# First half's residual through ScalarE and one accumulating DMA, VectorE's single steps in front of its up additions, scales in three tiles

## The chip, the cores and the metric

The kernel runs on one core of one Trainium2 chip. The metric is the device time of one execution in microseconds (us); the median of repeated runs is what counts. The core has TensorE (PE) for matmuls into the eight PSUM banks, VectorE (DVE), ScalarE (ACT) and GpSimd (POOL) for elementwise work, and 16 DMA engines. DMAs are issued by SyncE (SP) and, where they add to what is there, by POOL.

## The reference

```python
x = x + attention(conv(x, cond, fside))            # before the stage of this case
f = dynamic_mix(x, cond)                           # 1x1 convolution with mixed weights
dequantize = (int_w - zeros) * scales              # one scale per group of 128 input rows
gate = silu(f @ gate_proj)                         # 512 -> 1792
up   = f @ up_proj                                 # 512 -> 1792
x = x + (gate * up) @ down_proj                    # 1792 -> 512
```

x has 32 x 32 = 1024 tokens of 512 values, float32. The change lies in the last four lines. The weights are integers less their zero points, held exactly in float16; each group of 128 inputs has its own scales, so a product over 512 inputs is four products over 128, each scaled and added in float32.

## The kernel before

After attention comes the feed-forward stage, the last 180 us. It is cut into 28 tiles (`TILES`): the 1792 hidden values in 14 blocks of 128 (`IC`), first for tokens 0 to 511 (the first half, tiles 0 to 13), then for tokens 512 to 1023 (tiles 14 to 27). Everything is transposed: values on partitions, 512 tokens along the row. Inputs and hidden values are split in a high and a low float16 part, so every product is two matmuls of 128x128 by 128x512. A tile n has:

- `gate(n)` on PE, four products, into banks 0 to 3. ACT scales products 0 and 2 out of PSUM (`scaled`, L1369), DVE scales 1 and 3 and adds them (`scaled`, L1929), POOL adds the two sums (`add_part`, L2191), ACT takes silu (`gate`, L1382).
- `up(n)` on PE, four products, into banks 0 to 2 and 7. ACT scales the first (`up_first`, L1397), DVE adds the other three (`up_added`, L1936). The next tile's gate products use the same banks, so PE's third gate product of tile n+1 waits for DVE's second up addition of tile n (L994).
- POOL multiplies the two (`hidden`), ACT and POOL split the result in high and low (`hidden_high`, `hidden_low`), and two tiles later (`LAG`) PE makes four products with the down weights (`down`, L1020). DVE scales and adds blocks 0 and 2 in `acc` (`down_added_to`, L1954); ACT scales blocks 1 and 3 into `dprod`, which has two buffers (`down_scaled`, L1415), and POOL issues a DMA that adds them in `acc` (`move_down`, L2207, 512 KB). Its landing is waited for by the next `move_down` and by ACT two tiles on, before it writes that buffer again (L1421).

Each engine runs its own list, written out by hand; in the loop over n the order is, on PE: gate(n), down(n-2) blocks 0 and 1, up(n), down(n-2) blocks 2 and 3. On DVE (L2011 to L2040): gate additions, down addition 0, up additions 1 and 2, down addition 2, up addition 3. On ACT (L1456 to L1479): down copy 3 of n-3, the two gate copies, down copy 1, `up_first`, `hidden_high`, silu. On POOL (L2281 to L2290): hidden(n-1), move_down(n-3), add_part(n), hidden_low(n-1). Between these stand single steps for the second half and for the residual:

- `mix_power(1)`, `hidden_bound(1)`, `hidden_diagonal(1)`, `hidden_power(1)` on DVE derive powers of two by which the second half's values are scaled. They stand at the head of tiles 5, 6 and 9.
- `rows_high` (ACT) and `rows_low` (DVE) split the second half's inputs, held in `fnat`, behind tiles 5, 7, 9, 11; SP then issues 16 transposing DMAs (L628), which `gate(14)` waits for.
- `turn_x(half, c)` (PE, L1059) transposes x into the bank `side`. For the second half ACT copies it into `acc` before any down product is there (`turned_x`). For the first half it is turned in tiles 16 and 17 and DVE adds it to the finished sums (`result`, L1977), block by block, and each turn waits for the one before it to be read (L1064). SP stores each block as it is done (L631).
- `later_scales` (ACT, tile 13) makes the second half's three sets of scales.

Of the kernel before, what the change touches and what calls it, by code (L numbers as in the profile page):

```python
# [11 lines left out]
KC = DM // P  # L12
# [15 lines left out]
MOVED = 16 * G  # L28
FIRST = 2
LAG = 2  # L30
ROWS = (5, 7, 9, 11)
TURN_X = (9, 10, 11, 12)
UNITS = 2 * HKV
EPS = 1e-6
MASKED = -1e30
# [56 lines left out]
def build(nc, x_in, xt_in, mask_in, fs_in, cond_in, cw_in, conv_in, wq_in, wkv_in, wo_in, w0_in, w1_in, w2_in, b2_in, mix_in, vec_in,  # L92
          gu_w_in, gu_z_in, gu_s_in, dn_w_in, dn_z_in, dn_s_in, const_in, sel_in, out):
    ctx = ExitStack()
    with ctx:
# [317 lines left out]
        l_acc = sem("l_acc")  # L413
        t_xT = sem("t_xT")
        a_xT = sem("a_xT")
        d_res = sem("d_res")


        norms = nc.dram_tensor("norms", (BQ, S, G, HQ), F32, kind="Internal").ap()
# [101 lines left out]
        def _(sp):  # L521
# [107 lines left out]
                                 fpair[S * b:S * b + S, t, :, :, :].rearrange("p k c n -> p (k c) n"),  # L629
                                 transpose=True).then_inc(l_fT, 16)  # L630
            for c in range(KC):  # L631
                sp.wait_ge(d_res, c + 1)
                sp.dma_start(out[:, c, tokens(0)], acc[:, 0, place(c), :]).then_inc(l_out, 16)
            for c in (0, 2, 1, 3):
                if c == 1:
# [8 lines left out]
        def _(pe):  # L644
# [392 lines left out]
            def last_downs():  # L1037

                n = TILES - 2
                pe.wait_ge(p_hlo, n + 1)  # L1040
                pe.wait_ge(d_res, KC)
                down_block(n, 1)
                pe.wait_ge(d_g, 2 * TILES)
                down_block(n, 0)
                pe.wait_ge(d_us, 3 * TILES - 1)
                down_block(n, 2)
                pe.wait_ge(d_us, 3 * TILES)
                down_block(n, 3)
                n = TILES - 1
                pe.wait_ge(d_hlo, 1)  # L1050
                pe.wait_ge(a_u, TILES)
                down_block(n, 1)
                down_block(n, 0)
                pe.wait_ge(d_dn, down_added(n - 2, 2))
                down_block(n, 2)
                pe.wait_ge(d_dn, down_added(n - 2, 3))
                down_block(n, 3)

            def turn_x(half, c):  # L1059

                if half == 0:
                    pe.wait_ge(a_xT, KC)
                    if c:
                        pe.wait_ge(d_res, c)  # L1064
                elif c:
                    pe.wait_ge(a_xT, c)
                else:
                    pe.wait_ge(d_y, HQ * UNITS)
                    pe.wait_ge(a_hm, 2)
                for t in range(HQ):  # L1070
                    last = nc.tensor.transpose(side[:, P * t:P * t + P], x[:, HQ * half + t, P * c:P * c + P], ident)
                last.then_inc(t_xT, 1)
# [21 lines left out]
            for n in range(2, TILES):  # L1094
                gate(n)
                if n >= LAG:
                    down(n - LAG, (0, 1))
                if n in (2, 3):
                    mix(2 * n)
                elif n in TURN_X:  # L1100
                    turn_x(1, n - TURN_X[0])
                elif n in (IC + LAG, IC + LAG + 1):
                    turn_x(0, 2 * n - 2 * IC - 2 * LAG)
                up(n)
                if n >= LAG:
                    down(n - LAG, (2, 3))
                if n in (2, 3):
                    mix(2 * n + 1)
                elif n == 4:
                    bound(1)  # L1110
                elif n == 5:
                    hidden_rows(1)
                elif n == 6:
# [7 lines left out]
        def _(act):  # L1121
# [247 lines left out]
            def scaled(n, g):  # L1369
                half, i = divmod(n, IC)  # L1370
                act.wait_ge(t_g, KC * n + g + 1)
                if i == 0 and g == 0:
                    act.wait_ge(a_fscl if half else p_fscl, 3 if half else 1)
                if n >= 2:
                    if g:
                        act.wait_ge(p_whole, n - 1)
                    else:
                        act.wait_ge(p_hlo, n - 1)
                A(part[:, n % 2, :] if g else whole[:, n % 2, :], bank[g][:, :], ACT.Copy,
                  scale=gscl[:, half, i, g:g + 1]).then_inc(a_g, 1)  # L1380
# [2 lines left out]
                act.wait_ge(p_whole, n + 1)  # L1383
                A(whole[:, n % 2, :], whole[:, n % 2, :], ACT.Silu).then_inc(a_silu, 1)

            def later_scales():
                act.wait_ge(p_fdown, 2)
                act.wait_ge(l_gus, 16)
                A(uscl[:, 1, :, :], gus[:, 1, :, :], ACT.Copy, scale=fdown[:, 1:2]).then_inc(a_fscl, 1)
                A(gscl[:, 1, :, :], gus[:, 0, :, :], ACT.Copy, scale=finv[:, 1:2]).then_inc(a_fscl, 1)  # L1390
                A(dsc[:, 1, :, :], dscl[:, :, :], ACT.Copy, scale=hdown[:, 1:2]).then_inc(a_fscl, 1)

            def hidden_scale(half):
                act.wait_ge(t_hx, 2 * half + 2)
# [2 lines left out]
            def up_first(n):  # L1397
                half, i = divmod(n, IC)
                act.wait_ge(t_u, KC * n + 1)
                if n == 0:  # L1400
                    act.wait_ge(p_fscl, 2)
                if n >= 2:
                    act.wait_ge(p_h, n - 1)
                A(exact[:, n % 2, :], up_bank(n, 0)[:, :], ACT.Copy, scale=uscl[:, half, i, 0:1]).then_inc(a_u, 1)  # L1404
# [10 lines left out]
            def down_scaled(n, c):  # L1415
                half, i = divmod(n, IC)
                act.wait_ge(t_dn, down_done(n, c))
                if n == TILES - 1:
                    act.wait_ge(p_acc, 1)
                elif n >= 3 and c == 1:  # L1420
                    act.wait_ge(l_acc, down_moved(n - 2))  # L1421
                A(dprod[:, n % 2, c // 2, :] if n else acc[:, 0, place(c), :], down_bank(n, c)[:, :], ACT.Copy,
                  scale=dsc[:, half, i, c:c + 1]).then_inc(a_dn, 1)
# [32 lines left out]
            for n in range(2, TILES):  # L1456
                if LAG < n <= DIRECT + LAG:
                    down_scaled(n - LAG - 1, 3)
                scaled(n, 0)
                if n == 3:  # L1460
                    mix_out(5)
                elif n == 4:
                    mix_out(7)
                scaled(n, 2)
                if n >= LAG:
                    down_scaled(n - LAG, 1)
                up_first(n)
                hidden_high(n - 1)
                if n in (2, 3):
                    mix_out(2 * n)  # L1470
                elif n in ROWS:
                    rows_high(ROWS.index(n))
                if n == 7:
                    hidden_scale(1)
                elif n in TURN_X:
                    turned_x(n - TURN_X[0])
                elif n == IC - 1:
                    later_scales()
                gate(n)  # L1479
            down_scaled(TILES - 2, 1)  # L1480
            hidden_high(TILES - 1)
# [5 lines left out]
        def _(dve):  # L1487
# [489 lines left out]
            def result(c):  # L1977

                dve.wait_ge(t_xT, KC + c + 1)
                if c % 2:  # L1980
                    dve.wait_ge(l_acc, down_moved(IC - 1))
                else:
                    dve.wait_ge(d_dn, down_added(IC - 1, c))
                V.tensor_tensor(acc[:, 0, place(c), :], side[:, :], acc[:, 0, place(c), :], ALU.add).then_inc(d_res, 1)

            probs_sum(UNITS - 1)
            mix_max(1)
            mix_max(2)
# [20 lines left out]
            add_outputs(UNITS - 1, 1, 3)  # L2009
            dve.wait_ge(p_fscl, 3)  # L2010
            for n in range(2, TILES):  # L2011
                if n == 5:
                    mix_power(1)
                    hidden_bound(1)
                elif n == 6:
                    hidden_diagonal(1)
                elif n == 9:
                    hidden_power(1)
                scaled(n, 1)
                if n in (IC + LAG + 1, IC + LAG + 2):  # L2020
                    result(2 * n - 2 * IC - 2 * LAG - 1)
                scaled(n, 3)
                if n >= LAG:
                    down_added_to(n - LAG, 0)
                if n == 3:
                    mix_max(4)
                    mix_max(5)
                elif n == 4:
                    mix_max(6)
                    mix_max(7)  # L2030
                if n in (IC + LAG, IC + LAG + 1):
                    result(2 * n - 2 * IC - 2 * LAG)
                up_added(n, (1, 2))
                if n >= LAG:
                    down_added_to(n - LAG, 2)
                up_added(n, (3,))
                if n in ROWS:
                    rows_low(ROWS.index(n))
                if n == TILES - 1:
                    last_hidden()  # L2040
            down_added_to(DIRECT, 3)
# [8 lines left out]
        def _(pool):  # L2050
# [156 lines left out]
            def move_down(n):  # L2207

                if n:
# [4 lines left out]
                    if n == IC:  # L2214
                        pool.wait_ge(a_xT, KC)
                    pool.dma_start(acc[:, half, 2:KC, :],
                                   dprod[:, n % 2, :, :], accum_op=ALU.add).then_inc(l_acc, 16)

            def add_down(n, c, before):
                pool.wait_ge(a_dn, down_evicted(n, c))  # L2220
                if before:
# [59 lines left out]
            for n in range(LAG, TILES):  # L2281
# [4 lines left out]
                hidden_low(n - 1)  # L2286
                if n == 8:
                    hidden_product(1)
                elif n == 10:
                    feature_scale(1)  # L2290
            add_down(DIRECT, 1, 0)
            pool.wait_ge(d_hlo, 1)
            add_down(TILES - 2, 1, 1)
# [64 lines left out]
```

## Time and profile before

| | us |
|---|---|
| median of 3 runs (lowest, highest) | 687.81 (687.43, 687.95) |
| profiled execution, whole | 686.33 |
| profiled execution, span | 684.5 |
| busy in the span: PE, DVE, ACT, POOL | 665.2, 559.3, 419.0, 453.5 |
| accumulating DMAs `acc<-dprod`: 24 of 512 KB, median issue to landing | 4.6 |
| granted TensorE clock, mean | 0.999 of full speed |

The profiled execution's own time is the span and 1.8 us around it, so an estimate from its rows is made against 686.33 and then carried to the median. In timelines a matmul of 512 columns is shown with 0.38 us, but the next one starts 0.215 us after it: the time between starts is what counts. DVE's and ACT's instructions overlap their neighbours by some 0.1 us in the same way.

### The profile page before, as it was taken

The numbers are of one execution on the slowest core, as the hardware profiler recorded it, in microseconds if no ns is written. First come the engines' busy times: TensorE is split into PE (matmuls) and PEld (weight loads), VectorE is DVE, ScalarE is ACT, GpSimd is POOL, SyncE is SP. The second block draws the span as 40 slices with busy tenths as digits, with TensorE's granted clock in tenths as the row PEclk, the third lists the DMA queues.
The fourth block names the chain that finished last, engine by engine and source line by source line (L and its number), as shares of the span: only waits on it lengthen the run. The fifth ranks groups of instructions, "written<-read, shape, count | busy, mean of one in ns | idle before, by whom it ended". The sixth has DMA issues, their size and how long they took to land.

```text
span 684.5 us, 14468 instructions
## 1 busy us (share of the span) xinstructions
PE 665.2 (97%) x5004; PEld 374.7 (55%) x5004; DVE 559.3 (82%) x843; ACT 419.0 (61%) x1259; POOL 453.5 (66%) x379
## 2 busy tenths in 40 slices
PE   9999999999999999999999999999979999999995
PEld 8766555656656565665646656565634434444442
DVE  5867878969878887986977898677776899899987
ACT  0488572844647375474656638446465777877874
POOL 0468874873776497287559538737537678877886
PEclk9999999999999999999999999999999999999999
DMA  7420354574376366427426734443300156656454
GB/s 268 176 90 1 130 147 97 128 213 83 87 145 198 78 154 203 105 61 225 115 69 164 204 87 102 125 89 95 56 2 0 32 108 120 112 109 139 93 101 115
DMA packets 98800, 79.15 MB, mean 116 GB/s; under 512 B 79521, under 2 KB 80065, under 8 KB 96577
## 3 DMA queue, kind: packets, MB, share of 16 engines
q1 hardware_dynamic: 94864, 65.97, 36.7%
q0 software_dynamic: 3456, 12.58, 9.8%
q8 instruction: 24, 0.39, 0.2%
q14 instruction: 24, 0.19, 0.1%
q10 hardware_dynamic: 432, 0.01, 0.0%
HBM read 48.01 MB, written 2.21 MB: 73 GB/s over the span
## 4 chain that ended last, share of the span: by engine, by line
PE 65%; DVE 11%; POOL 10%; issue 7%; ACT 3%; DMA 3%; POOLq 0%; DVEq 0%; ACTq 0%
PE bank L651 17%; PE bank L653 17%; PE bank L652 17%; DMA acc<-dprod 3%; DVE exact L1945 3%; PE bank L703 2%; POOL wqlo L2069 2%; PE bank L841 1%; DVE mx L1533 1%; PE bank L1011 1%; PE bank L1012 1%; PE bank L995 1%; POOL qn L2105 1%; POOL whole L2193 1%; PE bank L1017 1%
## 5 line engine op out<-in xcount | busy, mean ns | idle before, releaser
L651 PE MATMUL bank<-wohi,oThi 128*128 128x512 f16 x256 | 97.1, 379 | 2.2 <-DVE oTlo L1721 2.1
L651 PE MATMUL bank<-wqhi,cThi 128*128 128x512 f16 x256 | 97.0, 379 | 0.9 <-POOL wqlo L2069 0.6
L653 PE MATMUL bank<-wohi,oTlo 128*128 128x512 f16 x256 | 97.0, 379 | 0.0
L652 PE MATMUL bank<-wolo,oThi 128*128 128x512 f16 x256 | 97.0, 379 | 0.0
L653 PE MATMUL bank<-wqhi,cTlo 128*128 128x512 f16 x256 | 97.0, 379 | 0.0
L652 PE MATMUL bank<-wqlo,cThi 128*128 128x512 f16 x256 | 97.0, 379 | 0.0
L1167 ACT ACTIVATE qraw<-bank 128x512 f32<-128x512 f32 x64 | 37.8, 591 | 81.5 <-PE bank L653 80.9
L2117 POOL TENSOR_TENSOR qinv<-qms,neghalf 128x8 f32<-128x8 f32 x28 | 56.9, 2030 | 39.6 <-ACT qms L1186 39.6
L2079 POOL TENSOR_TENSOR wolo<-wor,wohi 128x512 f16<-128x512 f32 x32 | 39.7, 1260 | 56.0 <-ACT wohi L1147 56.0
L1178 ACT ACTIVATE qsq<-qraw 128x128 f32<-128x128 f32 x256 | 75.4, 299 | 1.7
L1729 DVE SCALAR_TENSOR_TENSOR x<-bank,ysc,x 128x512 f32<-128x512 f32 x64 | 47.1, 744 | 30.6 <-PE bank L653 30.5
L1945 DVE SCALAR_TENSOR_TENSOR exact<-bank,uscl,exact 128x512 f32<-128x512 f32 x84 | 62.7, 746 | 10.5 <-ACT exact L1404 6.8
L651 PE MATMUL bank<-wkvhi,cThi 128*128 128x256 f16 x256 | 69.9, 273 | 0.0
L653 PE MATMUL bank<-wkvhi,cTlo 128*128 128x256 f16 x256 | 69.8, 273 | 0.0
L652 PE MATMUL bank<-wkvlo,cThi 128*128 128x256 f16 x256 | 69.8, 273 | 0.0
L2105 POOL TENSOR_TENSOR qn<-qraw,down 128x512 f16<-128x512 f32 x56 | 65.3, 1166 | 5.2 <-ACT qraw L1167 5.0
L2069 POOL TENSOR_TENSOR wqlo<-wqr,wqhi 128x512 f16<-128x512 f32 x32 | 37.8, 1213 | 25.9 <-ACT wqhi L1133 25.9
L1678 DVE SCALAR_TENSOR_TENSOR qn<-qraw,qn 128x512 f16<-128x512 f32 x56 | 46.4, 837 | 10.3 <-POOL qn L2105 10.2
L2198 POOL TENSOR_TENSOR whole<-whole,exact 128x512 f32<-128x512 f32 x27 | 36.2, 1339 | 21.7 <-DVE exact L1945 20.5
L1178 ACT ACTIVATION_READ_ACCUMULATOR qsq<-qraw 128x1 f32 x256 | 48.8, 191 | 0.0
L1017 PE MATMUL bank<-hT,dints 128*128 128x512 f16 x112 | 42.4, 379 | 2.5 <-DVE hT L1974 1.4
L1011 PE MATMUL bank<-fT,uint 128*128 128x512 f16 x112 | 42.6, 380 | 1.9 <-DVE whole L1934 1.7
(225 smaller groups left out, 1794.3 us busy)
## 6 DMA issues: line engine op xcount, KB each, us to landing
acc<-dprod POOLq DMA_DIRECT2D x24, 512.0 KB, 4.6
wqr<-in_wq SPq DMA_DIRECT2D x8, 1024.0 KB, 7.4
wor<-in_wo SPq DMA_DIRECT2D x8, 1024.0 KB, 6.0
raw<-in_gu_w SPq DMA_DIRECT2D x28, 256.0 KB, 3.2
zeros<-in_gu_z SPq DMA_DIRECT2D x28, 256.0 KB, 4.5
wkvr<-in_wkv SPq DMA_DIRECT2D x8, 512.0 KB, 7.2
raw<-in_dn_w SPq DMA_DIRECT2D x14, 256.0 KB, 2.7
zeros<-in_dn_z SPq DMA_DIRECT2D x14, 256.0 KB, 3.5
```

What stands on the lines that cost most here:

```text
L651: mm(o, ahi, bhi, start=start and k == 0, stop=False)
L652: mm(o, ahi, blo, start=False, stop=False)
L653: last = mm(o, alo, bhi, start=False, stop=stop and k == n - 1)
L1011: mm(o, uint[:, i, c, :], fThi[:, c, tokens(half)], start=True, stop=False)
L1017: mm(o, ints, hThi[:, n % (LAG + 1), :], start=True, stop=False)
L1178: A(qsq[:, t % 2, g, :], qraw[:, t, g, :], ACT.Square, accum_out=qss[:, g, t:t + 1]).then_inc(a_qss, 1)
L1678: V.scalar_tensor_tensor(qpair[:, t, 1, :, :], qraw[:, t, :, :], V_DOWN, qpair[:, t, 0, :, :], ALU.mult, ALU.subtract).then_inc(d_qlo, 1)
L1729: V.scalar_tensor_tensor(x[:, q, :], PC[t][:, :], ysc[:, half:half + 1], x[:, q, :], ALU.mult, ALU.add).then_inc(d_y, 1)
L1945: V.scalar_tensor_tensor(u, up_bank(n, c)[:, :], uscl[:, half, i, c:c + 1], u, ALU.mult, ALU.add).then_inc(d_us, 1)
L2069: Q.tensor_tensor(wqlo[:, c, :], wqr[:, c, :], wqhi[:, c, :], ALU.subtract).then_inc(p_wq, 1)
L2105: Q.tensor_tensor(qpair[:, t, 0, :, :], qraw[:, t, :, :], down[:, :, None].broadcast_to([P, G, HD]), ALU.mult).then_inc(p_qhi, 1)
L2117: Q.tensor_tensor(qinv[:, :, pair], qms[:, :, pair], neghalf[:, :, pair], ALU.pow).then_inc(p_qpow, 1)
```

## The change

- The four `result` additions of DVE are gone. ACT copies each turned block of x from the bank into `fnat` (`residual`), which is free by then: in tile 16 before silu, in 17 behind the first gate copy and before silu, in 18 behind the first gate copy. When all four are there, POOL issues one accumulating DMA of the whole `fnat` (1 MB) onto the first half of `acc`, behind `hidden_low(19)` in tile 20. SP's four stores all wait for its landing. PE waits for ACT's copies where it waited for DVE's additions.
- On DVE the single steps of tiles 5 and 6 stand behind the first down addition and before the up additions; `hidden_power(1)` also, and in tile 10 instead of 9. `rows_low` stands there too, one tile after its `rows_high`, which moves from tiles 5, 7, 9, 11 to 6, 7, 8, 10.
- The second half's turns of x move from tiles 9 to 12 to 9, 11, 12, 13.
- The later scales: gate scales in tile 8, up scales in tile 13, down scales in tile 14, with waits of their own. `feature_scale(1)` of POOL moves from tile 10 to 11.

```diff
-ROWS = (5, 7, 9, 11)
-TURN_X = (9, 10, 11, 12)
+ROWS = (6, 7, 8, 10)
+TURN_X = (9, 11, 12, 13)
...  SP
             for c in range(KC):
-                sp.wait_ge(d_res, c + 1)
+                sp.wait_ge(l_res, 16)
                 sp.dma_start(out[:, c, tokens(0)], acc[:, 0, place(c), :]).then_inc(l_out, 16)
...  PE, last_downs and turn_x
-                pe.wait_ge(d_res, KC)
+                pe.wait_ge(a_res, KC)
...
-                        pe.wait_ge(d_res, c)
+                        pe.wait_ge(a_res, c)
...  ACT
+            def residual(c):
+                act.wait_ge(t_xT, KC + c + 1)
+                act.wait_ge(d_fTlo, KC + HQ)
+                A(fnat[:, place(c), :], side[:, :], ACT.Copy).then_inc(a_res, 1)
...
                 scaled(n, 0)
+                if n in (IC + LAG + 1, IC + LAG + 2):
+                    residual(2 * n - 2 * IC - 2 * LAG - 1)
...
+                if n == LAG + 6:
+                    later_gate_scales()
                 elif n == IC - 1:
-                    later_scales()
+                    later_up_scales()
+                elif n == IC:
+                    later_down_scales()
+                elif n in (IC + LAG, IC + LAG + 1):
+                    residual(2 * n - 2 * IC - 2 * LAG)
                 gate(n)
...  DVE
             for n in range(2, TILES):
-                if n == 5:
-                    mix_power(1)
-                    hidden_bound(1)
-                elif n == 6:
-                    hidden_diagonal(1)
-                elif n == 9:
-                    hidden_power(1)
                 scaled(n, 1)
-                if n in (IC + LAG + 1, IC + LAG + 2):
-                    result(2 * n - 2 * IC - 2 * LAG - 1)
                 scaled(n, 3)
                 if n >= LAG:
                     down_added_to(n - LAG, 0)
...
-                if n in (IC + LAG, IC + LAG + 1):
-                    result(2 * n - 2 * IC - 2 * LAG)
+                elif n == 5:
+                    mix_power(1)
+                    hidden_bound(1)
+                elif n == 6:
+                    hidden_diagonal(1)
+                elif n == 10:
+                    hidden_power(1)
+                if n - 1 in ROWS:
+                    rows_low(ROWS.index(n - 1))
                 up_added(n, (1, 2))
                 if n >= LAG:
                     down_added_to(n - LAG, 2)
                 up_added(n, (3,))
-                if n in ROWS:
-                    rows_low(ROWS.index(n))
...  POOL
+            def add_residual():
+                pool.wait_ge(a_res, KC)
+                pool.wait_ge(d_dn, down_added(IC - 1, 2))
+                pool.wait_ge(l_acc, down_moved(IC - 1))
+                pool.dma_start(acc[:, 0, :, :], fnat[:, :, :], accum_op=ALU.add).then_inc(l_res, 16)
...
-                elif n == 10:
+                elif n == 11:
                     feature_scale(1)
+                elif n == IC + LAG + 4:
+                    add_residual()
```

## Rows read from the trace of the kernel before

**Rows 1.** The page: busy time by engine, then the chain that ended last.
```profile
PE 665.2 (97%) x5004; PEld 374.7 (55%) x5004; DVE 559.3 (82%) x843; ACT 419.0 (61%) x1259; POOL 453.5 (66%) x379
...
PE 65%; DVE 11%; POOL 10%; issue 7%; ACT 3%; DMA 3%; POOLq 0%; DVEq 0%; ACTq 0%
```
**Rows 2.** Windows, tile 22: us; PE, PEld, DVE, ACT, POOL busy; PEclk, DMA share, GB/s.
```profile
640.90:646.08 5.18, 5.18 (x26) 2.33 (x25) 4.81 (x8) 4.22 (x7) 4.43 (x6) 1.00 0.51 97
```
**Rows 3.** Timeline of PE, tiles 5 and 6: start, us, instruction, [idle <-releaser].
```profile
544.09 0.38 PE L995 MATMUL bank<-fT,gint 128*128 128x512 f16 x1 [0.26 <-DVE exact L1945]
...
546.03 0.38 PE L1012 MATMUL bank<-fT,uint 128*128 128x512 f16 x1
...
546.90 0.39 PE L1011 MATMUL bank<-fT,uint 128*128 128x512 f16 x1 [0.49 <-DVE whole L1934]
...
552.08 0.38 PE L1012 MATMUL bank<-fT,uint 128*128 128x512 f16 x1
...
553.50 0.39 PE L1011 MATMUL bank<-fT,uint 128*128 128x512 f16 x1 [1.05 <-DVE whole L1934]
```
**Rows 4.** Timeline of DVE, tiles 5 and 6.
```profile
545.18 0.15 DVE L1892 TENSOR_REDUCE fsum<-bank 128x1 f32<-128x5 f32 x1
...
546.09 0.75 DVE L1934 SCALAR_TENSOR_TENSOR whole<-bank,gscl,whole 128x512 f32<-128x512 f32 x1 [0.30 <-issue]
...
550.90 0.74 DVE L1926 SCALAR_TENSOR_TENSOR fpair<-fnat,fup,fpair 128x512 f16<-128x512 f32 x1
551.56 0.27 DVE L1906 TENSOR_REDUCE hrow<-bank 4x1 f32<-4x128 f32 x1
551.87 0.92 DVE L1907 TENSOR_SCALAR hdiag<-const,hrow 4x4 f32<-4x4 f32 x1
552.71 0.73 DVE L1934 SCALAR_TENSOR_TENSOR whole<-bank,gscl,whole 128x512 f32<-128x512 f32 x1
```
**Rows 5.** Timeline of DVE, first up additions of tiles 7 and 11.
```profile
560.34 1.60 DVE L1945 SCALAR_TENSOR_TENSOR exact<-bank,uscl,exact 128x512 f32<-128x512 f32 x2 [0.46 <-ACT exact L1404]
...
583.28 1.60 DVE L1945 SCALAR_TENSOR_TENSOR exact<-bank,uscl,exact 128x512 f32<-128x512 f32 x2 [0.57 <-ACT exact L1404]
```
**Rows 6.** Timeline of DVE, tile 17, and of PE beside it.
```profile
615.29 0.68 DVE L1984 TENSOR_TENSOR acc<-bank,acc 128x512 f32<-128x512 f32 x1
...
615.58 0.38 PE L1018 MATMUL bank<-hT,dints 128*128 128x512 f16 x1
616.12 0.63 PE L1071 MATMUL bank<-const,x 128*128 128x128 f32 x4 [0.16 <-DVE acc L1984]
```
**Rows 7.** Timeline of ACT: the first of the scales, and waits in tiles 13, 16 and 22.
```profile
595.05 0.34 ACT L1389 ACTIVATE uscl<-gus,fdown 128x56 f32<-128x56 f32 x1
...
596.06 0.63 ACT L1384 ACTIVATE whole<-whole 128x512 f32<-128x512 f32 x1 [0.20 <-POOL whole L2193]
...
612.49 0.63 ACT L1384 ACTIVATE whole<-whole 128x512 f32<-128x512 f32 x1 [0.47 <-POOL whole L2193]
...
643.69 0.69 ACT L1422 ACTIVATE dprod<-bank,dsc 128x512 f32<-128x512 f32 x1 [0.28 <-PE bank L1018]
```
**Rows 8.** Timeline of POOL, tiles 20 to 22.
```profile
635.48 1.45 POOL L2204 TENSOR_TENSOR hT<-whole,hT 128x512 f16<-128x512 f32 x1
...
637.54 1.27 POOL L2198 TENSOR_TENSOR whole<-whole,exact 128x512 f32<-128x512 f32 x1 [0.61 <-DVE exact L1945]
...
638.76 0.88 POOL L2216 DMA_DIRECT2D acc<-dprod  x1
...
644.02 0.87 POOL L2216 DMA_DIRECT2D acc<-dprod  x1
```
**Rows 9.** Windows, from one accumulating DMA's issue to the next.
```profile
638.76:643.99 5.23, 5.23 (x25) 2.24 (x24) 4.91 (x8) 4.03 (x8) 4.48 (x5) 1.00 0.53 100
```
**Rows 10.** Tile acc: landing times of all its DMAs, then the stores' line.
```profile
DMA to landing us min/median/max: 2.1/4.5/5.5
...
result<-acc SPq DMA_DIRECT2D x8, 256.0 KB, 2.1
```

More of the change, by code:

```diff
@@ L415, in build @@
         a_xT = sem("a_xT")
-        d_res = sem("d_res")
+        a_res = sem("a_res")
+        l_res = sem("l_res")
         norms = nc.dram_tensor("norms", (BQ, S, G, HQ), F32, kind="Internal").ap()
@@ L1100, in _ @@
                 elif n in TURN_X:
-                    turn_x(1, n - TURN_X[0])
+                    turn_x(1, TURN_X.index(n))
                 elif n in (IC + LAG, IC + LAG + 1):
@@ L1372, in scaled @@
                 if i == 0 and g == 0:
-                    act.wait_ge(a_fscl if half else p_fscl, 3 if half else 1)
+                    act.wait_ge(a_fscl if half else p_fscl, 1)
                 if n >= 2:
@@ L1384, in gate, with later_gate_scales, later_up_scales, later_down_scales @@
                 A(whole[:, n % 2, :], whole[:, n % 2, :], ACT.Silu).then_inc(a_silu, 1)
-            def later_scales():
+            def later_gate_scales():
+                act.wait_ge(d_fup, 2)
+                act.wait_ge(l_gus, 16)
+                A(gscl[:, 1, :, :], gus[:, 0, :, :], ACT.Copy, scale=finv[:, 1:2]).then_inc(a_fscl, 1)
+            def later_up_scales():
                 act.wait_ge(p_fdown, 2)
-                act.wait_ge(l_gus, 16)
                 A(uscl[:, 1, :, :], gus[:, 1, :, :], ACT.Copy, scale=fdown[:, 1:2]).then_inc(a_fscl, 1)
-                A(gscl[:, 1, :, :], gus[:, 0, :, :], ACT.Copy, scale=finv[:, 1:2]).then_inc(a_fscl, 1)
+            def later_down_scales():
                 A(dsc[:, 1, :, :], dscl[:, :, :], ACT.Copy, scale=hdown[:, 1:2]).then_inc(a_fscl, 1)
+            def residual(c):
+                act.wait_ge(t_xT, KC + c + 1)
+                act.wait_ge(d_fTlo, KC + HQ)
+                A(fnat[:, place(c), :], side[:, :], ACT.Copy).then_inc(a_res, 1)
             def hidden_scale(half):
@@ L1399, in up_first @@
                 act.wait_ge(t_u, KC * n + 1)
-                if n == 0:
-                    act.wait_ge(p_fscl, 2)
+                if i == 0:
+                    act.wait_ge(a_fscl if half else p_fscl, 2)
                 if n >= 2:
@@ L1417, in down_scaled @@
                 act.wait_ge(t_dn, down_done(n, c))
+                if n == IC:
+                    act.wait_ge(a_fscl, 3)
                 if n == TILES - 1:
@@ L1475, in _ @@
                 elif n in TURN_X:
-                    turned_x(n - TURN_X[0])
+                    turned_x(TURN_X.index(n))
+                if n == LAG + 6:
+                    later_gate_scales()
                 elif n == IC - 1:
-                    later_scales()
+                    later_up_scales()
[3 more added lines that the diff above has]
+                    residual(2 * n - 2 * IC - 2 * LAG)
                 gate(n)
@@ L1975, in hidden_low @@
                                 ALU.subtract).then_inc(d_hlo, 1)
[L1977 to L1984, printed above, removed]
             probs_sum(UNITS - 1)
```

## The prediction

> **What bounds the kernel now.** I read the page first. TensorE is busy for 97% of the span and VectorE for 82%, and the chain that ended last lies on PE for 65% [rows 1]. The change touches only the two-layer feed-forward stage, tiles 2 to 27, so I read windows and timelines there. A tile without disturbance takes 5.18 us: PE is busy throughout, VectorE 4.81 us of it, ScalarE 4.22, GpSimd 4.43, and the clock is granted in full, which is 2.4 GHz [rows 2]. So this stage is bound by PE's 24 matmuls (0.215 us from start to start), with VectorE only 0.37 us behind, and time can be won only where PE stands still. The views to look at are therefore PE's timeline, for pitches over 0.215, and the neighbours' rows beside each. I found such pitches in tiles 5 and 6 (the largest), in 17, and small ones in tiles 8 to 16, 21 and 26.
>
> **Single steps moved (the vector loop's head to before the up additions).** In tile 5 `mix_power(1)` and `hidden_bound(1)` occupy VectorE from 545.18 to 546.09, so the gate addition starts 0.9 us late [rows 4], and PE goes from 546.03 to 546.90, a pitch of 0.87, that is 0.65 us lost [rows 3]. In tile 6 the low rows of tile 5 (550.90, 0.66 to the next start) and `hidden_diagonal(1)` (551.56 to 552.71, 1.15) stand ahead of the gate addition [rows 4]. PE goes from 552.08 to 553.50 [rows 3]: 1.42 less 0.215 is 1.20 lost. The change takes both away: 1.85 us. But the instructions stay, now in front of the up additions. Those hold another matmul: the third gate matmul of the next tile reuses the bank of the second up addition, and PE has waited for just that at 544.09 [rows 3]. With 0.9 us in front in tile 5, up additions start at about 548.06, as before, and the second ends near 549.7, while PE, 0.65 us ahead, would want the bank at 549.5: 0.2 to 0.3 come back. In tile 6, 1.15 us in front make it about 0.5. I take 1.85 - 0.75 = 1.1 us. Ends: nothing (VectorE's sum is unchanged and only 0.37 us per tile is free [rows 2]) and the 1.85.
>
> The low rows move from the end of tiles 5, 7, 9, 11 to the middle of 7, 8, 9, 11. Before the first up addition VectorE stood idle waiting for ScalarE, 0.46 us in tile 7 and 0.57 in tile 11 [rows 5] (three such tiles, the third, 9, with less). That covers two thirds of each 0.66. The small PE losses they caused disappear, but rows in two tiles running (7 and 8) make new ones of about 0.3. Their input on ScalarE (`rows_high`) moves by one tile, and the 16 transposes on SP's queue start later and end earlier; the second half needs them only at tile 14. `hidden_power(1)` moves from tile 9 to 10, the x turns by one or two tiles; neither is waited for before tile 13. For all this I take 0.3 us gained; ends -0.5 and +0.8.
>
> **Residual off VectorE.** Four additions of 0.68 us, pitch 0.60 [rows 6], leave VectorE in tiles 16 to 18: 2.4 us. But these tiles have PE work added (the turns), and PE stood still only once: from 615.58 to 616.12, waiting for the addition at 615.29 [rows 6], 0.54 less 0.215 is 0.32 us. ScalarE's copy of that block comes just after its first gate copy, earlier than the addition did, so the 0.32 goes. What is late next is PE itself. The four copies cost ScalarE at most 0.69 each, as its copy of another bank does [rows 7], in front of waits that it has anyway (0.47 us for GpSimd in tile 16 [rows 7]). Gain 0.3; ends 0.3 below zero (a copy that makes `silu` late) and 1.1, were VectorE's relief to reach tiles 19 to 21.
>
> **Scales in three tiles.** All three ran between 595.05 and 596.06, and the `silu` behind them then still waited 0.20 us for GpSimd [rows 7]. Split, they are still under the same wait in tiles 8, 13 and 14: nothing; uncovered, 0.2 each way.
>
> **The accumulating DMA.** This is the cost. GpSimd issues one DMA of 1 MB behind `hidden_low(19)`, at about 636.8 [rows 8]. It runs in a gap of 0.61 us (the next addition starts at 637.54), about the time that an issue holds GpSimd, so the issue itself is free. Next in the same queue is `move_down(18)`, issued at 638.76 [rows 8]. The trace has only accumulating DMAs of 512 KB. Between one issue and the next the DMA engines are busy for 0.53 of 5.23 us, 2.8 us [rows 9]; issue to landing is 4.5 [rows 10], so 1.7 is fixed. Twice the bytes, in order in the one queue: residual 636.8 + 1.7 + 5.6 = 644.1, and tile 18's product after it at 644.1 + 2.8 = 646.9. ScalarE's `down_scaled(20, 1)` writes the buffer that this DMA reads; it started at 643.69 and had waited only for PE [rows 7]. So it is now 3.2 us late. Behind it on ScalarE stand `up_first(22)`, `hidden_high(21)` and `silu`; VectorE's up additions wait for the first, and PE for those. GpSimd's `move_down(19)`, at 644.02 [rows 8], waits for the same landing, and `add_part(22)` stands behind it. PE has no slack to give back at 5.18 a tile. The stores of the first half, four of 256 KB, now all leave when the residual lands, instead of one by one in tiles 16 to 18; alone each takes 2.1 us [rows 10]. They share the engines with tile 18's and 19's products: 0.3 more. Cost 3.5 us. Ends: if a packet of twice the bytes took no longer, 636.8 + 1.7 + 2.8 + 2.8 = 644.1, 0.4 us late; if each 512 KB took what the longest landing has, 5.5 - 1.7 = 3.8, then 649.9, 6.2 late.
>
> The Trainium skill (DMA: Bandwidth & Descriptors, "Anatomy of one DMA") fits a GpSimd-issued DMA by 2.0 us plus bytes over 436 GB/s. The same page ("SWDGE vs HWDGE vs iDMA") says that only one software queue is allocated, which is what makes the product wait behind the residual. The fit would give the 512 KB landing 3.2 us; the trace disagrees, with 4.5 [rows 10]. By that fit the residual takes 2.4 us of transfer and the cost would be near zero, the first rival below.
>
> **Sum.** Gains 1.1 + 0.3 + 0.3 = 1.7, cost 3.5: 1.8 us slower. The profiled execution took 686.33, so 688.1 by its own time; the median of the runs shown is 687.81, 1.5 above it, so 689.6.
>
> **Rivals.** *The residual hides (faster).* DMA engines are idle 47% of a tile [rows 9]. If the transfer of 1 MB takes at most about 3 us, tile 18's product lands by 644.1, and only 0.4 of the gains is lost: 687.81 - 1.7 + 0.4 = 686.5. It decides from a landing of the residual before about 641.4. Against it: the share in [rows 9] is near full while the engines move, so bytes seem to be what they wait for. Chance 0.2. *The two cancel.* The gain at tiles 5 and 6 comes whole (1.85 + 0.6 = 2.5) and the delay is 2.5, because engines have begun tile 18's product early: 687.8. Chance 0.22. *Nothing won in front.* VectorE's sum per tile bounds tiles 5 to 9, the moved steps only change which wait is last, and the full delay is paid: 687.81 + 3.5 = 691.3. For it: 0.37 us of slack [rows 2] against 3 us of single steps. Against it: the two long waits of PE are for exactly the additions that come first now. Chance 0.16. The forecast has 0.42.
>
> **Numbers.** Likeliest 689.6, its own range 688.5 to 690.8. The range takes in the hidden residual and the last rival: 686.1 to 691.4. A measurement of this kernel can tell about 0.2%, 1.4 us, from no change. Faster by more: 0.19, half of the first rival (its 686.5 stands at the bound of 686.4) and as much again from cases with both a hidden residual and more of the ends named above. Within: 0.25, the cancelling case and the edges of both neighbours. Slower: 0.56.
>
> **What would show it.** PE's second up matmul of tiles 5 and 6 follows its neighbour at 0.215, and the third gate matmuls of tiles 6 and 7 wait for the up addition instead. The DMA into acc from fnat lands 7 to 7.5 us after its issue, and the next from dprod 8 us after its own instead of 4.5. ScalarE's dprod copy in tile 22 waits for it about 3 us, and PE shows one hole of about that size in tiles 22 and 23. No PE wait is left in tile 17. I am wrong if the residual lands in under 5 us, or if tiles 5 to 8 take as long as before.

## The result

| | median, us | ratio to the kernel before, 95% interval |
|---|---|---|
| before | 687.88 (687.43 to 688.81, 4 runs) | |
| changed | 698.47 (695.61 to 698.76, 4 runs) | 1.0143 [1.0127, 1.0159] |

The changed kernel is 10.6 us slower. The direction was forecast, the size was not: 1.8 us were expected, and 698.47 lies far outside 686.1 to 691.4. The profiled execution took 698.52, its span is 696.7 (12.2 more than before; 1.0 of that is there at the first gate matmul, in a part that the change doesn't touch).

I first made the same sum for both traces: for each tile, how long PE stood still, as the time between matmul starts over 0.215 us. (Tiles 5 to 26: 6.7 us before, 17.8 after. Such a loss is called a hole below. Tiles that are not listed have at most 0.2 us in either.)

| tile | 5 | 6 | 7 | 8 | 10 | 12 | 14 | 15 | 17 | 21 | 22 | 23 | 24 | 26 |
|---|---|---|---|---|---|---|---|---|---|---|---|---|---|---|
| before | 1.26 | 1.40 | 0 | 0.36 | 0.22 | 0.24 | 0.71 | 0.86 | 0.32 | 0.47 | 0 | 0 | 0.07 | 0.56 |
| changed | 0.51 | 1.59 | 0.41 | 4.47 | 2.36 | 3.98 | 0 | 0 | 0 | 0.48 | 1.87 | 1.13 | 0.78 | 0 |

Two places are worse: tiles 6 to 13, by 10.5 us, and 22 to 24, by 3.7. Other tiles are better, by 3.1 in all. The page of the changed kernel shows one effect of it, 8.1 us in which gate matmuls waited for VectorE's up additions (L1967; 1.1 before), but has no line for either cause. That line, and the busy time by engine, which answers to [rows 1]:

```profile
L996 PE MATMUL bank<-fT,gint 128*128 128x512 f16 x112 | 43.7, 390 | 8.2 <-DVE exact L1967 8.1
...
PE 670.7 (96%) x5004; PEld 377.2 (54%) x5004; DVE 566.0 (81%) x839; ACT 421.7 (61%) x1263; POOL 451.9 (65%) x380
```

VectorE has four instructions fewer (839 for 843) and 6.7 us more of busy time. That is the first clue: some instruction has become longer. VectorE's timeline of the changed kernel in tiles 6, 7 and 8 (start, us, instruction), which answers to [rows 4]:

```profile
553.84 0.27 DVE L1928 TENSOR_REDUCE hrow<-bank 4x1 f32<-4x128 f32 x1
554.14 2.22 DVE L1929 TENSOR_SCALAR hdiag<-const,hrow 4x4 f32<-4x4 f32 x1
...
561.08 3.25 DVE L1948 SCALAR_TENSOR_TENSOR fpair<-fnat,fup,fpair 128x512 f16<-128x512 f32 x1
...
569.05 2.12 DVE L1948 SCALAR_TENSOR_TENSOR fpair<-fnat,fup,fpair 128x512 f16<-128x512 f32 x1
```

`rows_low` took 0.74 us at 550.90 [rows 4]; here it takes 3.25, 2.12, 3.27 and 2.94. The 4x4 product of `hidden_diagonal` took 0.92 and takes 2.22. GpSimd's timeline at the same times:

```profile
553.66 1.57 POOL L2202 TENSOR_TENSOR whole<-whole,part 128x512 f32<-128x512 f32 x1
554.88 1.45 POOL L2213 TENSOR_TENSOR hT<-whole,hT 128x512 f16<-128x512 f32 x1
...
561.10 1.56 POOL L2202 TENSOR_TENSOR whole<-whole,part 128x512 f32<-128x512 f32 x1
562.34 1.43 POOL L2213 TENSOR_TENSOR hT<-whole,hT 128x512 f16<-128x512 f32 x1
...
569.06 1.54 POOL L2202 TENSOR_TENSOR whole<-whole,part 128x512 f32<-128x512 f32 x1
571.13 1.16 POOL L2213 TENSOR_TENSOR hT<-whole,hT 128x512 f16<-128x512 f32 x1 [0.52 <-ACT hT L1425]
```

Set the ends beside each other. At 561 GpSimd runs two instructions on end, until 563.8, and VectorE's ends at 564.33, about 0.6 us later, which is its own length. At 569 GpSimd's second comes only after a wait, and VectorE is done at 571.17, 0.6 us after the first (570.60). So VectorE stood in line behind GpSimd, and started when GpSimd paused. (At 561 its row even starts 0.02 us before GpSimd's; which of two starts that close came first can't be read from a trace.)

The trace of the kernel before had shown this already, in its attention stage, at a line that the prediction didn't look at. It also has two inputs in SBUF, and a constant where `rows_low` has the column `fup`. Its durations are shortest, median and longest, in ns; then one case beside GpSimd:

```profile
L1678 DVE SCALAR_TENSOR_TENSOR qn<-qraw,qn x56: 627/692/2853, 89.1 to 481.0; 128x512 f16<-128x512 f32 x56
```
```profile
181.91 2.72 POOL L2079 TENSOR_TENSOR wolo<-wor,wohi 128x512 f16<-128x512 f32 x2
...
183.59 1.58 DVE L1678 SCALAR_TENSOR_TENSOR qn<-qraw,qn 128x512 f16<-128x512 f32 x1
184.58 1.49 POOL L2105 TENSOR_TENSOR qn<-qraw,down 128x512 f16<-128x512 f32 x1
```

GpSimd's pair ends at 184.63 and VectorE at 185.17, 0.54 later. There VectorE got its turn although GpSimd's next instruction followed at once; at 561 it did not. The runs don't show what makes the difference.

PE paid for the long `rows_low`, because the up additions behind it free the banks. PE's timeline at the head of tile 8, with [rows 3] to compare:

```profile
565.13 0.38 PE L996 MATMUL bank<-fT,gint 128*128 128x512 f16 x1 [2.21 <-DVE exact L1967]
...
565.99 0.38 PE L996 MATMUL bank<-fT,gint 128*128 128x512 f16 x1 [0.26 <-DVE exact L1967]
```

And then PE ran slowly. Windows of 2 us (PE busy, number of matmuls in brackets; the granted clock is the third number from the end), for [rows 2]:

```profile
562.00:564.00 2.00, 0.93 (x5) 0.20 (x2) 2.00 (x1) 1.70 (x5) 1.76 (x2) 1.00 1.08 205
564.00:566.00 2.00, 0.60 (x3) 0.17 (x4) 1.90 (x4) 0.55 (x1) 0.00 (x0) 1.00 0.38 69
566.00:568.00 2.00, 2.00 (x7) 0.80 (x8) 2.00 (x4) 0.69 (x1) 0.76 (x1) 0.66 0.20 34
568.00:570.00 2.00, 2.00 (x6) 0.64 (x5) 2.00 (x3) 0.84 (x2) 2.00 (x3) 0.50 0.53 94
570.00:572.00 2.00, 2.00 (x11) 0.91 (x10) 1.90 (x3) 2.00 (x5) 1.48 (x2) 0.99 1.07 195
```

PE was busy for 1.5 of 4 us, and then got 1.2 GHz instead of 2.4 for some 3 us, twice in this stage (also at 594 to 597, tile 12). Eight matmuls of tile 8 each came 0.2 us late, 1.6 of its 4.47, and eight of tile 12, 1.6 of its 3.98.

The hole of tile 6 comes by another path, which the prediction doesn't name: PE itself waits for the 4x4 product (`hdiag`), which it multiplies in this tile.

```profile
556.42 0.38 PE L967 MATMUL bank<-hdiag,spread 4*128 4x4 f32 x2 [1.32 <-DVE hdiag L1929]
```

The second place is the one that was forecast. ScalarE's waits for the product's landing in tiles 22 and 23, then the DMAs' issues on GpSimd, then landing times from a view of the DMAs between 645.6 and 658 [rows 7, 8, 10]:

```profile
655.57 0.69 ACT L1436 ACTIVATE dprod<-bank,dsc 128x512 f32<-128x512 f32 x1 [2.88 <-DMA acc<-dprod]
...
661.54 0.69 ACT L1436 ACTIVATE dprod<-bank,dsc 128x512 f32<-128x512 f32 x1 [0.85 <-DMA acc<-dprod]
```
```profile
645.61 1.17 POOL L2233 DMA_DIRECT2D acc<-fnat  x1
...
647.80 1.12 POOL L2225 DMA_DIRECT2D acc<-dprod  x1
...
656.03 0.89 POOL L2225 DMA_DIRECT2D acc<-dprod  x1 [2.95 <-DMA acc<-dprod]
```
```profile
acc<-fnat POOLq DMA_DIRECT2D x1, 1024.0 KB, 7.3
acc<-dprod POOLq DMA_DIRECT2D x2, 512.0 KB, 6.6
```

The residual lands 7.3 us after its issue, as worked out (1.7 + 5.6), and ScalarE waits 2.9, against 3.2. The 6.6 is the median of two products: the next `move_down`, at 656.03, had waited for the first of them, issued at 647.80, so that one took about 8.2, against 8 forecast.

### The profile page after: what moved, and what is told of

The parts are those of the page before. It is cut to its first block, busy times and chain, and to the rows that moved or that the text cites. A ratio compares the mean times of both kernels' runs of the same rounds, so it can differ in the third digit from the quotient of the medians.

```text
span 696.7 us, 14471 instructions
## 1 busy us (share of the span) xinstructions
PE 670.7 (96%) x5004; PEld 377.2 (54%) x5004; DVE 566.0 (81%) x839; ACT 421.7 (61%) x1263; POOL 451.9 (65%) x380
## 4 chain that ended last, share of the span: by engine, by line
PE 71%; DVE 9%; POOL 9%; issue 6%; DMA 3%; ACT 2%; POOLq 0%; DVEq 0%; ACTq 0%
PE bank L652 17%; PE bank L654 17%; PE bank L653 17%; DMA acc<-dprod 3%; PE bank L704 2%; PE bank L996 2%; DVE exact L1967 2%; PE bank L997 2%; POOL wqlo L2078 2%; PE bank L1012 2%; PE bank L1018 2%; PE bank L1013 2%; PE bank L1019 2%; PE bank L842 1%; POOL whole L2202 1%
## 5 line engine op out<-in xcount | busy, mean ns | idle before, releaser
L2126 POOL TENSOR_TENSOR qinv<-qms,neghalf 128x8 f32<-128x8 f32 x28 | 55.2, 1971 | 39.1 <-ACT qms L1187 39.1
L1967 DVE SCALAR_TENSOR_TENSOR exact<-bank,uscl,exact 128x512 f32<-128x512 f32 x84 | 62.7, 747 | 14.3 <-ACT exact L1416 10.7
L2207 POOL TENSOR_TENSOR whole<-whole,exact 128x512 f32<-128x512 f32 x27 | 34.6, 1283 | 32.0 <-DVE exact L1967 30.8
L996 PE MATMUL bank<-fT,gint 128*128 128x512 f16 x112 | 43.7, 390 | 8.2 <-DVE exact L1967 8.1
```

Source lines behind the costliest of these rows:

```text
L996: mm(bank[g][:, :], gint[:, i, g, :], fThi[:, g, tokens(half)], start=True, stop=False)
L1967: V.scalar_tensor_tensor(u, up_bank(n, c)[:, :], uscl[:, half, i, c:c + 1], u, ALU.mult, ALU.add).then_inc(d_us, 1)
L2126: Q.tensor_tensor(qinv[:, :, pair], qms[:, :, pair], neghalf[:, :, pair], ALU.pow).then_inc(p_qpow, 1)
```

## The experiments

Theory: VectorE's instructions that read two operands in SBUF do not run while GpSimd runs its own on SBUF. Rivals: the longer instructions wait for data (ScalarE, transposes), VectorE's total load is what counts, or the big DMA is most of it.

**e1, rows back.**
```diff
-ROWS = (6, 7, 8, 10)
+ROWS = (5, 7, 9, 11)
...
-                if n - 1 in ROWS:
-                    rows_low(ROWS.index(n - 1))
                 up_added(n, (1, 2))
...
                 up_added(n, (3,))
+                if n in ROWS:
+                    rows_low(ROWS.index(n))
```


> The changed kernel with rows_high and rows_low back where they were (tiles 5, 7, 9, 11, rows_low behind the last up addition); all else as changed. Theory A (VectorE's rows_low, which reads two tensors of SBUF, is held up while GpSimd runs its own instructions on SBUF; at the end of a tile GpSimd is idle): the four rows_low take 0.74 us instead of 2.1 to 3.3, PE's holes of 4.5, 2.4 and 4.0 us in tiles 8, 10 and 12 go, about 8 of the 10.6 us come back: 690 to 691. Rival B (the extra time is VectorE's own load, which is only 0.37 us per tile under PE's, so moving it does not matter): 697 or more. Rival C (the accumulating DMA of the residual is most of the loss): 696 to 698.

Measured 690.45, ratio to before 1.0038 [1.0027, 1.0050]: 8.0 of the 10.6 us come back. The rows take 0.74 each. The three large holes are gone. The 4x4 product stayed where the change put it and still takes 2.19. VectorE has the same instructions to run as in the changed kernel, so its load is not what counts. VectorE's timeline of e1, and GpSimd's, show both sides:

```profile
552.07 0.74 DVE L1948 SCALAR_TENSOR_TENSOR fpair<-fnat,fup,fpair 128x512 f16<-128x512 f32 x1
...
555.00 2.19 DVE L1929 TENSOR_SCALAR hdiag<-const,hrow 4x4 f32<-4x4 f32 x1
```
```profile
552.23 1.71 POOL L2207 TENSOR_TENSOR whole<-whole,exact 128x512 f32<-128x512 f32 x1 [0.85 <-DVE exact L1967]
```

At the end of a tile VectorE comes first, and it is GpSimd that waits: its product takes 1.71 instead of 1.27 [rows 8].

**e2, one input in PSUM.** Only `rows_low`, at the changed place:
```diff
+                dve.wait_ge(t_u, KC * n + 2)
-                V.scalar_tensor_tensor(fpair[:, t, 1, :, :], fnat[:, t, :]..., fup[:, 1:2],
+                V.scalar_tensor_tensor(fpair[:, t, 1, :, :], up_bank(n, 1)[:, :]..., V_DOWN,
                                        fpair[:, t, 0, :, :], ALU.mult, ALU.subtract)
```


> The changed kernel with rows_low at its new place, its first input a PSUM bank (the tile's second up product) instead of fnat: same shape, same output and second input; the low parts of the second half's inputs are thereby not what the reference has. Theory A: one input less in SBUF, so it is not held up: 0.75 us each though it stands at the same place, and the time is 690 to 692, as with rows_low at the end. Rival B (it waits for ScalarE's rows_high, or SP's transposes of fpair hold it): still 2.1 to 3.3 us each, 697 to 699.

Measured 690.06, ratio 1.0043 [1.0026, 1.0059]. The instruction's line in the view of its output:

```profile
L1950 DVE SCALAR_TENSOR_TENSOR fpair<-bank,fpair x4: 680/682/691, 560.7 to 582.9; 128x512 f16<-128x512 f32 x4
```

Same place, same waits for ScalarE and the same transposes of its output, 0.68 us (shortest, median and longest are 680, 682 and 691 ns). The low rows it makes are not those of the second half's inputs; only their time counts here. The rival that it waits for data has fallen.

The edit takes away two operands in SBUF, the tensor `fnat` and the column `fup`, so by itself it doesn't say which of them counts. Two other rows do: `qn<-qraw,qn` of the kernel before has a constant for the column and was held up, and the up additions (`exact<-bank,uscl,exact`, one input in PSUM, a column and a tensor in SBUF) start in the middle of GpSimd's `add_part` in e9 (561.45, below) and take their usual time. So it is the second tensor in SBUF that makes it wait. The 690.06 holds 4.7 us of holes in tiles 22 to 24, with a fall of the clock at 648 to 651, against 3.8 in the changed kernel.

**e8, the rows alone.** The kernel before with the move of the rows (the constants and the place) and nothing else.

> The kernel before with one part of the change alone: rows_high in tiles 6, 7, 8, 10 and rows_low one tile later in front of the up additions. Theory (held up by GpSimd's instructions there): rows_low takes 2 to 3.3 us, PE's holes as in the changed kernel, clock falls to 1.2 GHz after the longest: 694 to 696. Rival (only together with the other moved steps): under 690.

Measured 692.94, ratio 1.0081 [1.0061, 1.0101]: 4.9 us for this part by itself, less than expected. The clock fell once (573 to 577) and not twice, and one of the rows, 1.70 us, was behind a single instruction of GpSimd. Its four rows in the view of their output:

```profile
L1926 DVE SCALAR_TENSOR_TENSOR fpair<-fnat,fup,fpair x4: 1699/2880/3249, 560.0 to 588.7; 128x512 f16<-128x512 f32 x4
```

**e9, the rows one instruction earlier.**
```diff
                 scaled(n, 3)
+                if n - 1 in ROWS:
+                    rows_low(ROWS.index(n - 1))
                 if n >= LAG:
                     down_added_to(n - LAG, 0)
...
-                if n - 1 in ROWS:
-                    rows_low(ROWS.index(n - 1))
```


> The changed kernel with rows_low one instruction earlier, in front of the first down addition instead of behind it, in the same tiles. There GpSimd has just multiplied and issued its DMA, and its next addition waits for the gate addition ahead of rows_low. Theory (VectorE is held up only while a GpSimd instruction is running when it starts): 0.74 us each instead of 2.1 to 3.3, no holes over 1 us in tiles 8 to 13, about 691 as e1, 0.66 us of position worth 7 us. Rival (any place in the middle of a tile costs it, because the two engines are both busy there): 696 or more.

Measured 688.62, ratio 1.0014 [1.0003, 1.0025]. One place earlier in VectorE's list is worth 9.9 us. VectorE and GpSimd in tile 7 of e9:

```profile
560.13 0.74 DVE L1948 SCALAR_TENSOR_TENSOR fpair<-fnat,fup,fpair 128x512 f16<-128x512 f32 x1
560.19 0.89 POOL L2225 DMA_DIRECT2D acc<-dprod  x1
560.79 0.74 DVE L1989 SCALAR_TENSOR_TENSOR acc<-bank,dsc,acc 128x512 f32<-128x512 f32 x1
560.80 1.58 POOL L2202 TENSOR_TENSOR whole<-whole,part 128x512 f32<-128x512 f32 x1
...
561.45 1.59 DVE L1967 SCALAR_TENSOR_TENSOR exact<-bank,uscl,exact 128x512 f32<-128x512 f32 x2
```

`rows_low` runs while GpSimd issues its DMA, and is nearly done when `add_part` starts. It beats even e1, which I had not expected: no tile from 12 to 16 has a hole left, where e1 has 2.2 us (and e5 and e6, with the same lists there, 1.3 and 1.4).

**e3, all single steps back.** e1, and `mix_power`, `hidden_bound`, `hidden_diagonal` at the head of tiles 5 and 6, `hidden_power` of 9:
```diff
+                if n == 5:
+                    mix_power(1)
+                    hidden_bound(1)
+                elif n == 6:
+                    hidden_diagonal(1)
+                elif n == 9:
+                    hidden_power(1)
                 scaled(n, 1)
```


> The changed kernel with all of VectorE's single steps back (rows_low, rows_high, mix_power, hidden_bound, hidden_diagonal, hidden_power); what stays is the residual through ScalarE and the 1 MB DMA, the scales, and the turns. Theory: only the DMA's delay is left, 2.9 us of ScalarE's wait in tile 22 and what follows, less 0.3 in tile 17: 690.5 to 691.5. Rival (the single steps other than rows_low won something in tiles 5 and 6): 0.5 to 1 above e1. Rival (the DMA costs nothing): 688.

Measured 690.77, ratio 1.0043 [1.0026, 1.0059]; e1 and e3 can't be told apart. In the traces tile 5's hole is 0.50 in e1 and 1.26 in e3, tile 6's 2.04 and 1.41. Tile 7 has 0.41 in e1 and none in e3. So `mix_power` in its new place wins 0.75, and `hidden_diagonal` in its new place loses 1.0: of the forecast gain of 1.1 us nothing is left.

**e4, the residual back on VectorE**, the rest as changed: `result` for `residual`, `d_res` for `a_res` and `l_res`, and
```diff
-                elif n == IC + LAG + 4:
-                    add_residual()
```


> The changed kernel with the residual as before (VectorE adds each turned block, SP stores it, no 1 MB DMA); single steps, rows, scales and turns as changed. Theory: the holes of tiles 22 to 24 (1.9, 1.1, 0.8 us of PE) go, about 3 us: 695 to 696. Rival (the DMA is harmless, all 10.6 us are the rows): 698.5.

Measured 693.92, ratio 1.0091 [1.0074, 1.0108]: 4.5 us less than changed, more than the 3 expected. Holes in tiles 22 to 24 are gone (0.08 left). The rest is in tiles 6 to 12, where its rows took 1.8 to 3.2 us but left 10.2 us of holes instead of 12.9; in it the clock fell twice as well, the first time at 559, right behind tile 6. VectorE's delays depend on where GpSimd happens to be. I can't say that this part belongs to the residual.

**e5, four DMAs.** e1 with
```diff
-                pool.dma_start(acc[:, 0, :, :], fnat[:, :, :], accum_op=ALU.add).then_inc(l_res, 16)
+                pool.dma_start(acc[:, 0, place(c), :], fnat[:, place(c), :], accum_op=ALU.add).then_inc(l_res, 16)
...
-                elif n == IC + LAG + 4:
-                    add_residual()
+                elif IC + LAG + 4 <= n < IC + LAG + 8:
+                    add_residual(n - IC - LAG - 4)
```


> e1 (the changed kernel with the rows at their old place) with the residual's DMA cut in four of 256 KB, one behind hidden_low in each of tiles 20 to 23, and each store waiting for its own. Theory (tile 18's product stands behind 1 MB in one queue; a quarter takes about 1.4 us of the 2.4 us that the engines are idle per tile): ScalarE's wait of 2.9 us in tile 22 goes, PE's holes of tiles 22 to 24 (3.8 us together) fall under 1: about 3 us less than e1, 687 to 688. Rival (the same bytes cost the same wherever they run, or the store burst is what hurts): within 1 of e1's 690.4.

Measured 687.81, ratio 1.0005 [0.9993, 1.0016]: 2.6 less than e1. The holes of tiles 22 to 24 are 0.19, 0.22 and 0.20. What is left there may be GpSimd's time for an issue, which holds back its next product by 1.0 us; no run shows it by itself. From its timeline of tile 20:

```profile
636.03 1.18 POOL L2236 DMA_DIRECT2D acc<-fnat  x1
637.06 1.45 POOL L2207 TENSOR_TENSOR whole<-whole,exact 128x512 f32<-128x512 f32 x1
```

**e6, stores late.** e1 with `sp.wait_ge(l_acc, down_moved(23))` ahead of the four stores.

> e1 with SP's four stores of the first half held back until tile 23's product has landed, so that no store runs while tiles 18 and 19 move. Theory: the hole in tile 22 (1.9 us) stays, since it is the 1 MB; those of 23 and 24 (1.1 and 0.8), where products share the engines with the stores, shrink: 0.5 to 1.5 less than e1, 689 to 690. Rival (the whole delay is the queue behind 1 MB): as e1, 690.4.

Measured 691.99, ratio 1.0060 [1.0045, 1.0074]: 1.5 more than e1, against both. Tiles 22 and 23 keep their holes (1.82, 1.12), so the stores have no part in those, and they are the queue behind 1 MB; tile 24's falls from 0.76 to 0.35. But the late stores (issued from 673.9 to 675.3) now meet the last product, which ends the kernel: ScalarE waits 3.42 us for it instead of 1.79.

```profile
680.69 0.69 ACT L1437 ACTIVATE dprod<-bank,dsc 128x512 f32<-128x512 f32 x1 [3.42 <-DMA acc<-dprod]
```

**e7, mended.** e5 with rows at the ends of tiles 6, 8, 9, 11, `hidden_all`, `hidden_scale` and `hidden_product` a tile later, and
```diff
                     down_added_to(n - LAG, 2)
+                if n == 6:
+                    hidden_row(1)
                 up_added(n, (3,))
+                if n == 6:
+                    hidden_spread(1)
```


> e5 with VectorE's steps placed where GpSimd stands idle: rows at the end of tiles 6, 8, 9, 11; hidden_diagonal cut in two (its reduction ahead of tile 6's last up addition, the 4x4 product right behind it), hidden_all, hidden_scale and hidden_product one tile later; mix_power in front of tile 5's up additions as changed. Theory: the 4x4 product takes 0.2 instead of 2.2 us, PE's hole in tile 6 (2.0 in e1) falls under 0.5: 1 to 2 us less than e5, 685.5 to 686.5, the first to beat the kernel before. Rival (VectorE's sum of work bounds tiles 5 to 9, so the hole only moves): as e5.

Measured 687.29, ratio 0.9992 [0.9980, 1.0005]; not told apart from e5 or before. The mechanism is as expected: the 4x4 product takes 0.2 us, tile 6's hole is 0.09. But tile 7's is 0.75 where e5 has 0.41, and the rows at the tiles' ends keep 1.4 us in tiles 14 and 15.

```profile
L1938 DVE TENSOR_SCALAR hdiag<-const,hrow x2: 208/213/218, 503.2 to 557.1; 4x4 f32<-4x4 f32 x2
```

**e10, e7 without the residual's part** (`result` on VectorE as before).

> e7 without the residual part: VectorE adds the turned blocks and SP stores them as in the kernel before, no DMA from fnat. It says what ScalarE's copies and the four small DMAs are worth once nothing stands behind 1 MB. Theory: 0.3 us of PE's wait in tile 17 against 0.8 of small holes in tiles 22 to 25: 0.3 to 0.6 less than e7, 686.8 to 687.1, faster than before by 0.1 to 0.2%. Rival (VectorE's relief of 2.4 us counts later): 1 us more than e7.

Measured 686.52, ratio 0.9983 [0.9973, 0.9994]: just faster than before. Its interval overlaps that of e7, so what ScalarE's copies and the small DMAs cost is not told apart from nothing.

**e11 and e12, both mended.** e10 and e7 with the rows as in e9:
```diff
-ROWS = (6, 8, 9, 11)
+ROWS = (6, 7, 8, 10)
```


> e10 with the rows as in e9 (rows_high in tiles 6, 7, 8, 10, rows_low one tile later in front of the first down addition). In e9 that place also left no hole in tiles 12 to 16, where the kernel before has 2.0 us. Theory: e10's holes of tiles 12 to 15 (2.4 us) go too: 1.5 to 2 less than e10, 684.5 to 685.2, clearly faster than before. Rival (those holes come from DMA landings that differ by chance): as e10, 686.5.

> e11 with the residual through ScalarE and four DMAs of 256 KB (e7 with the rows as in e9). Theory: 0.3 to 0.8 more than e11, as e7 stood to e10 (the small DMAs cost GpSimd and the queue a little in tiles 22 to 25): 685.0 to 685.8. Rival (VectorE's relief of 2.4 us is worth something once the other holes are gone): less than e11.

Measured 685.15, ratio 0.9956 [0.9941, 0.9972], and 685.66, ratio 0.9962 [0.9949, 0.9975] (before: 688.22 beside them). e11 beats both kernels: 3.1 us under the one before, 13.3 under the changed one. Its holes in tiles 5 to 26 sum to 3.1 us (0.3 in tiles 12 to 15); e12's to 3.9. The two can't be told apart by time, so VectorE's relief of 2.4 us is worth nothing here that the runs show.

Holes of PE by stretch, us:

| | median | tiles 6 to 13 | 14, 15 | 22 to 24 |
|---|---|---|---|---|
| before | 687.9 | 2.4 | 1.6 | 0.1 |
| changed | 698.5 | 12.9 | 0 | 3.8 |
| e1 | 690.4 | 4.7 | 1.3 | 3.8 |
| e9 | 688.6 | 3.4 | 0 | 3.8 |
| e5 | 687.8 | 3.7 | 1.3 | 0.6 |
| e11 | 685.1 | 1.5 | 0.3 | 0.4 |

## Why the prediction was wrong

- **What bounds the kernel.** Right: PE at 5.18 us a tile, and the losses are holes in PE's row (11.1 us more of them in tiles 5 to 26, beside 10.6 in the median). All sums above are made that way.
- **The low rows, "covers two thirds of each 0.66", gain 0.3 with ends -0.5 and +0.8.** This is the step that failed. It took the instruction's 0.74 us along to its new place. That figure came from a place where GpSimd stands idle; the new place is the start of two GpSimd instructions in a row (`add_part`, `hidden_low`), and I read GpSimd's timeline only for the residual's DMA. The instruction took 2.1 to 3.3 us there. The runs put 8.0 us (e1) to 9.9 us (e9) on it. About 3.2 of that is the clock, 1.6 us each in tiles 8 and 12. By itself on the kernel before it costs 4.9 (e8). The Trainium skill (SBUF — State Buffer, "Who interferes with whom") states it: a VectorE instruction with two SBUF inputs and a GpSimd instruction that reads SBUF share a read port, and whichever issues second waits. I had not drawn on it. e2 agrees, 0.68 us with one input in PSUM against 2.1 to 3.3 with two in SBUF. The Trainium skill (SBUF — State Buffer, "Summary: rules for kernel authors") says that the second waits until the first finishes. The attention stage agrees (185.17, behind the instruction that ended at 184.63); in this stage VectorE waited through two on end (3.25 us), and through one where GpSimd paused (2.12).
- **Single steps, "I take 1.85 - 0.75 = 1.1 us".** Wrong in sum: e1 and e3 differ by nothing that can be told. `mix_power` won 0.75 in tile 5 (0.65 forecast). `hidden_diagonal` was counted at 1.15 in front of the up additions and took 2.5: 0.27 and 2.22, the same cause; and PE waited for its result directly (1.32 us in tile 6), which is in no term. Its 0.92 at the head [rows 4] was a warning that I read as the instruction's own length; in e7, with GpSimd idle when it starts, it is 0.21.
- **The accumulating DMA, "Cost 3.5 us".** Right. Landing 7.3 forecast and measured; ScalarE's wait 3.2 and 2.9; holes of tiles 22 to 24 3.8 in the changed kernel, and 2.6 us won back by four DMAs (e5). That stores add to it was right in tile 24 (0.4), not in 23. The issue was taken as free in a gap of 0.61 us; it held GpSimd 0.97 (645.61 to 646.58). By the fit of the Trainium skill (DMA: Bandwidth & Descriptors, "Anatomy of one DMA"), 2.0 us plus bytes over 436 GB/s, the estimate for 1 MB is 4.4 us, which would have made it nearly free; the trace disagrees, with 7.3.
- **Residual off VectorE, 0.3.** Tile 17's 0.32 went, as forecast. That it is worth anything in the time isn't shown (e11 and e12 can't be told apart).
- **Not forecast:** the holes of tiles 14 and 15 (1.6 us) go with the rows in earlier tiles. I had them in no term. e8, which moves only the rows, has 0.3 left there, so it is the rows and no other part of the change. Whether that is because the transposes of `fpair` end sooner, and no longer share the DMA engines with the products, was not tried by itself; e1 and e5, with the rows late, keep 1.3, e9 and e11, with them early, 0 to 0.3.

Without the low rows' term the total would have come out near the measured one: 2.1 forecast (the 1.8, and the 0.3 that they were to win), 2.5 and 2.8 measured for e1 and e3 above the kernel before, in which the low rows stand where they were. For e1 that is in part luck, since the 1.1 us of the single steps are in its forecast and not in its trace.

## What to carry to other kernels

An instruction's duration belongs to the place where it was measured. Before a VectorE instruction with two SBUF operands is moved, look at what GpSimd runs at the new time: between GpSimd's instructions (idle, or issuing a DMA) it costs its own length, at their start it costs theirs too. A line of one shape whose durations spread from 0.6 to 2.9 us, as L1678's did before the change, is a sign that they depend on what runs beside it. And a transfer put into a queue is paid by the next one in it: cut it to what the engines' idle time per period holds (e5: 2.6 us back).

## What was not expected of the hardware

- A VectorE product of 4x4 elements, of a tensor and a column in SBUF, took 2.22 us beside GpSimd and 0.21 without. Steps of one element per partition with constants (`hdown`, 0.14 and 0.15 us at 583.88 and 584.06 in the changed kernel) were not held up though GpSimd ran from 583.90, nor were the up additions, which read a column and a tensor in SBUF beside their bank. Which property of the operands decides for the 4x4 product is left open.
- GpSimd is held for 0.6 us by the issue of a product's DMA (560.19 to 560.80 in e9) and for 1.0 by that of 256 KB from `fnat` (636.03 to 637.06 in e5), and a VectorE instruction on two SBUF tensors runs unhindered during the first (0.74 us, also in e11, where `rows_low` starts at 558.57, 0.27 after the issue).
- In the changed kernel the granted clock fell to 0.50 in tile 8, after PE had been busy 1.5 of 4 us, and in tile 12. Tiles 10 and 12 each have a hole of 1.93 us and PE busy for 2.0 of the 4 us around it (577 to 581, 590 to 594); the clock fell in 12 and not in 10. In e4 it fell behind a hole of 1.5 us (tile 6). What decides is not shown by these runs.
